# Slot stage: the normalisation ahead of attention, layers and gate moves from ScalarE (with shifts from VectorE) to GpSimd

## The reference

```python
slots = q_mu + jnp.exp(q_logsig) * noise          # noise = layernorm(x)
for _ in range(3):
    prev = slots
    q = _ln(slots, lnq_g, lnq_b) @ wq + bq         # norm "q"
    logits = jnp.einsum('bnd,bkd->bnk', k, q) / scale
    attn = jax.nn.softmax(logits, axis=-1) + 1e-8
    attn = attn / jnp.sum(attn, axis=1, keepdims=True)
    upd = jnp.einsum('bnk,bnd->bkd', attn, v)
    slots = upd @ wu + bu + prev
    h = _ln(slots, lnm_g, lnm_b) @ w1 + b1         # norm "m"
    slots = jax.nn.gelu(h) @ w2 + b2 + slots
    slots = _ln(slots + x_cls[:, None, :], lnp_g, lnp_b)   # norm "o"
...
x = x + slots
x = x + experts_b(_layernorm(x, axis=-1))          # norm "q" of a fourth round
```

## Time and profile before

| | |
|---|---|
| time, median of 3 runs | 892.08 us (891.86 to 893.96) |
| the profiled execution | 893.99 us, span of its instructions 892.1 us |
| busy in the span | PE 766.4 us, DVE 568.9, ACT 529.1, POOL 364.6 |
| busy, 700.8 to 743.5 us | PE 33.88, DVE 35.90, ACT 38.19, POOL 12.13 |
| mean granted TensorE clock | 0.918 of full speed |

### The profile page before, as it was taken

The page is one execution under the profiler, slowest core; times in us unless marked ns, Lnnn a source line. Parts: engine busy times, 40 slices in busy tenths (PEclk is TensorE's granted clock), DMA queues, the critical chain, the costliest instruction groups (busy, mean ns, idle before and its releaser), DMA issues.

```text
span 892.1 us, 17850 instructions
## 1 busy us (share of the span) xinstructions
PE 766.4 (86%) x5685; PEld 640.3 (72%) x5685; DVE 568.9 (64%) x1970; ACT 529.1 (59%) x1144; POOL 364.6 (41%) x571
## 2 busy tenths in 40 slices
PE   5989799999999999999988978999948787862793
PEld 4766687788887888777767656999836565752793
DVE  1657877788686667777765663343499888885012
ACT  3654567676666766666665542333549888851472
POOL 1323544343342334233336653565542232327362
PEclk9999999999999999999998979999957979785797
DMA  9424404360710520120232024888520000001674
GB/s 249 125 76 132 165 1 148 97 224 1 240 59 24 164 82 1 53 53 7 71 134 63 28 79 145 243 253 247 166 80 1 1 1 0 1 1 49 165 208 131
DMA packets 82054, 88.52 MB, mean 99 GB/s; under 512 B 6155, under 2 KB 69851, under 8 KB 81323
## 3 DMA queue, kind: packets, MB, share of 16 engines
q1 hardware_dynamic: 78475, 80.19, 30.3%
q0 software_dynamic: 3488, 7.20, 2.2%
HBM read 69.03 MB, written 35.17 MB: 117 GB/s over the span
## 4 chain that ended last, share of the span: by engine, by line
PE 58%; DVE 20%; ACT 9%; issue 5%; POOL 4%; DMA 3%; SPq 1%; DVEq 0%; POOLq 0%; ACTq 0%
PE bank L713 6%; PE bank L1036 6%; PE bank L707 5%; PE bank L740 4%; DVE sb_smax L1542 4%; PE bank L780 3%; DVE sb_row_sum L1551 3%; PE bank L1044 3%; PE bank L845 3%; PE bank L749 2%; PE bank L1145 2%; PE bank L765 2%; PE bank L1153 2%; POOL sb_expd L2066 2%; PE bank L722 2%
## 5 line engine op out<-in xcount | busy, mean ns | idle before, releaser
L2066 POOL TENSOR_TENSOR sb_expd<-sb_expd,sb_rden 128x512 f32<-128x512 f32 (+1 forms) x128 | 111.3, 870 | 248.4 <-DVE sb_rden L1555 248.3
L1542 DVE TENSOR_REDUCE sb_smax<-bank 128x4 f32<-128x512 f32 (+1 forms) x128 | 74.2, 580 | 75.9 <-PE bank L740 40.4
L1273 ACT ACTIVATE sb_expd<-sb_shifted 128x512 f32<-128x512 f32 (+1 forms) x128 | 69.7, 545 | 42.6 <-DVE sb_shifted L1545 41.6
L2158 POOL TENSOR_TENSOR sb_rstd_all<-sb_rsq_all,sb_halves 128x4 f32<-128x4 f32 x44 | 45.0, 1023 | 108.8 <-DVE sb_rsq_all L1893 108.6
L1551 DVE TENSOR_REDUCE sb_row_sum<-sb_expd 128x4 f32<-128x512 f32 (+1 forms) x128 | 73.0, 570 | 7.7 <-ACT sb_expd L1273 7.6
L1545 DVE TENSOR_TENSOR sb_shifted<-bank,sb_smax 128x512 f32<-128x512 f32 (+1 forms) x128 | 75.0, 586 | 4.4
L707 PE MATMUL bank<-sb_h1T,sb_watt 128*128 128x128 f32 x512 | 70.5, 289 | 4.6 <-DMA sb_watt<-att_w 2.9
L707 PEld LDWEIGHTS bank<-sb_h1T,sb_watt 128*128 128x128 f32 x512 | 64.6, 202 | 7.3 <-DMA sb_watt<-att_w 3.3
L1036 PE MATMUL bank<-sb_blk_xT,sb_up_w 128*128 128x128 f32 x456 | 57.1, 275 | 0.0
L1036 PEld LDWEIGHTS bank<-sb_blk_xT,sb_up_w 128*128 128x128 f32 x456 | 54.0, 192 | 0.0
L1855 DVE TENSOR_TENSOR sb_hid<-bank,sb_hid 128x384 f32<-128x384 f32 x38 | 21.2, 558 | 51.1 <-ACT sb_hid L1321 51.1
(11 more groups left out here) (285 smaller groups left out, 1997.9 us busy)
## 6 DMA issues: line engine op xcount, KB each, us to landing
sb_up_w<-gate_up SPq DMA_DIRECT2D x38, 384.0 KB, 4.3
sb_v<-v_all SPq DMA_DIRECT2D x16, 576.0 KB, 6.6
rows_b<-pad_b SPq DMA_DIRECT2D x7, 1105.0 KB, 10.1
rows_a<-pad_a SPq DMA_DIRECT2D x7, 975.0 KB, 8.3
sb_up_w<-w1b SPq DMA_DIRECT2D x23, 256.0 KB, 3.7
v_all<-sb_moe_w SPq DMA_DIRECT2D x14, 308.0 KB
sb_blk_x<-rows_a SPq DMA_DIRECT2D x38, 65.0 KB, 3.2
sb_picked<-back_a SPq DMA_DIRECT2D x4, 512.0 KB, 5.5
```

The costliest lines, as they stand in the source:

```text
L1273: act.activation(exp_of(i, s, j), shifted[:, u % 2, :, 0:n], ACT.Exp, scale=DH ** -0.5).then_inc(exp_done, 1)
L1542: dve.tensor_reduce(smax[:, u % 2, :], s_in, X, ALU.max).then_inc(max_done, 1)
L2066: pool.tensor_tensor(e, e, rden[:, u % 2, :].unsqueeze(2).broadcast_to([P, QH, n]), ALU.mult).then_inc(norm_done, 1)
```

## The change

The steps `norm_q` and `norm_m` leave ScalarE's queue for GpSimd's, and the steps `shift_q` and `shift_m` leave VectorE's altogether, with their semaphore. GpSimd waits for its own root and then runs one instruction a tile, (x - mean) * rstd, reading `mv_all` and `rstd_all` as per-partition scalars. TensorE waits for the same semaphore as before, now raised by GpSimd. The phases of `norm_q` and `norm_m` become those of their roots plus 0.0005, so each stands right behind its root in GpSimd's queue. No other phase changes. (Line numbers of the new kernel are its own: the root is L2137 there, the normalisation L2142, scaling L1354, exponentials L1365, shares L1371, Gelu L1377, bias L2150, scatter L2014.)

```diff
@@ SLOT_STEPS
-        "norm_q": (0.5900, 0.3921, 0.5369, 0.4138),
+        "norm_q": (-14.4877, -14.6377, -14.8345, -13.9260),
-        "norm_m": (2.9165, 2.4781, 2.0449, 2.1655),
+        "norm_m": (-12.5585, -11.6081, -12.5116, -12.9450),
@@ ScalarE
-            def normed(it, g, k, src, dst):
-                act.wait_ge(shift_ready[k], nth("shift_" + k, it, g))
-                for b in tiles(g):
-                    ins = act.activation(dst[:, b, 0:D], src[:, b, :], ACT.Identity, scale=rstd_all[:, b:b + 1],
-                                         bias=nbias[:, b:b + 1])
-                ins.then_inc(z_normed[k], 1)
@@ VectorE
-            def shifted_by(it, g, k):
-                c = slice(4 * g, 4 * g + 4)
-                dve.wait_ge(root_ready[k], nth("root_" + k, it, g))
-                dve.scalar_tensor_tensor(nbias[:, c], mv_all[:, c, 0], -1.0, rstd_all[:, c], ALU.mult, ALU.mult).then_inc(
-                    shift_ready[k], 1)
@@ GpSimd
-            for step, it, g in slot_steps("bias_u", "root_q", "root_m", "root_o", "send"):
+            def normed(it, g, k, src, dst):
+                pool.wait_ge(root_ready[k], nth("root_" + k, it, g))
+                for b in tiles(g):
+                    ins = pool.tensor_scalar(dst[:, b, 0:D], src[:, b, :], mv_all[:, b, 0:1], rstd_all[:, b:b + 1],
+                                             ALU.subtract, ALU.mult)
+                ins.then_inc(z_normed[k], 1)
+
+            for step, it, g in slot_steps("bias_u", "root_q", "root_m", "root_o", "send", "norm_q", "norm_m"):
...
+                if step == "norm_q":
+                    normed(it, g, "q", *((S, zs) if it < SLOT_ITERS else (x_sb, sent[0])))
+                if step == "norm_m":
+                    normed(it, g, "m", S, zs)
```

More of the change, by code:

```diff
@@ L492, in program @@
         var_ready, root_ready = ({k: sem(f"sl_{n}_{k}") for k in "qmo"} for n in ("var_ready", "root_ready"))
-        shift_ready, z_normed = ({k: sem(f"sl_{n}_{k}") for k in "qm"} for n in ("shift_ready", "z_normed"))
+        z_normed = {k: sem("sl_z_normed_" + k) for k in "qm"}
         zT_done, zT_ready = ({k: sem(f"sl_{n}_{k}") for k in "qm"} for n in ("zT_done", "zT_ready"))
@@ L1361, in scaled @@
                 act.activation(group_of(zsT, g), bank[2 * g][:, :], ACT.Identity, scale=scale, bias=bias).then_inc(zT_ready[k], 1)
-            for step, it, g in slot_steps("norm_q", "scale_q", "exp", "shares", "norm_m", "scale_m", "gelu", "choice_exp"):
-                if step == "norm_q":
-                    normed(it, g, "q", *((S, zs) if it < SLOT_ITERS else (x_sb, sent[0])))
+            for step, it, g in slot_steps("scale_q", "exp", "shares", "scale_m", "gelu", "choice_exp"):
                 if step == "scale_q" and it < SLOT_ITERS:
@@ L1381, in _ @@
                     ins.then_inc(att_ready, 1)
-                if step == "norm_m":
-                    normed(it, g, "m", S, zs)
                 if step == "scale_m":
@@ L1893, in measured @@
                 dve.scalar_tensor_tensor(rsq_all[:, 0, c], mv_all[:, c, 1], 1.0, eps[:, c], ALU.mult, ALU.add).then_inc(var_ready[k], 1)
-            def shifted_by(it, g, k):
-                c = slice(4 * g, 4 * g + 4)
-                dve.wait_ge(root_ready[k], nth("root_" + k, it, g))
-                dve.scalar_tensor_tensor(nbias[:, c], mv_all[:, c, 0], -1.0, rstd_all[:, c], ALU.mult, ALU.mult).then_inc(
-                    shift_ready[k], 1)
             of_b = [routing("b", part) for part in range(len(PARTS["b"]))]
             dve.wait_ge(exp_out["a"], len(PARTS["a"]) + 1)
-            for step, it, g in slot_steps("add", "measure_q", "shift_q", "max", "share_sum", "updated", "measure_m", "shift_m",
+            for step, it, g in slot_steps("add", "measure_q", "max", "share_sum", "updated", "measure_m",
                                           "measure_o", "centre", "slots", "gated", "choose", "place"):
@@ L1916, in _ @@
                     measured(g, x_sb, "q")
-                if step == "shift_q":
-                    shifted_by(it, g, "q")
                 if step == "max":
@@ L1938, in _ @@
                     measured(g, S, "m")
-                if step == "shift_m":
-                    shifted_by(it, g, "m")
                 if step == "measure_o":
```

## The result

The changed kernel takes 923.42 us (median of 4 runs, 917.5 to 925.31), against 892.08 before: a ratio of 1.0343 [1.03, 1.0386] with its 95% interval, 31 us slower and far outside the forecast range of 884.5 to 897.5. One further execution of the kernel before took 1126.62 us, far above all others, and is not counted. The changed kernel's profiled execution took 923.88 us with a span of 922.1.

What follows compares the result with a forecast made beforehand. No single engine was taken as full: four groups chase each other through four in-order queues. Laps -2.7, first delay +1.1 and tail +0.4 sum to -1.2 us, from 892.08 to 890.9 us; range 884.5 to 897.5.

Steps and rivals of the forecast that it cites:

- I take 0.40, nearer the upper row: Price of GpSimd's new instruction: 0.40 us a tile, chosen between a copy's 0.29 and a two-tensor addition's 0.45.
- I add nothing there: In a lap, a root delayed behind a normalisation on GpSimd costs nothing, since its slots run only at 740.35.
- likeliest case: Whole kernel: VectorE takes over what ScalarE lets go, change under 0.3%, 889.4 to 893 us; chance 0.40.
- first delay: Stage start: the first normalisation holds up the next group's output root on GpSimd, so VectorE's slots start later: +1.1 us.
- tail: Stage end: the last normalisation stands ahead of GpSimd's twelve scatters, so loads of scattered rows start later: +0.4 us.
- the laps' -2.7: Slot-loop laps: Gelu on ScalarE no longer waits behind the normalisation, 0.9 us gained at each of three lap ends.
- faster rival: Whole kernel: a tile costs 0.30 us and more of ScalarE's relief arrives, -5 us, 887; chance 0.33.
- dear instruction: GpSimd: at 0.90 us a tile a group takes 3.6 us and GpSimd becomes the bound: +7 us, 899; chance 0.15.
- Seven paths 1 us longer: Slow case at 0.90 us a tile: seven normalisation paths each lengthen by 1 us.
- It decides from about 0.65 a tile: GpSimd price from which the slow case holds: a path is as long as the mean now and roots queue.
- instructions that fall under a normalisation: VectorE: some 6 small instructions a lap wait a mean of 0.2 us for GpSimd, 1.2 us, even with removed shifts.
- a rival of its own: VectorE's slots also alternate with GpSimd's tiles, 11 hits of up to 0.4 us a lap: +4.5 us, 895; chance 0.12.

Runs made afterwards that it cites:

- run 4: Not a name in the kept text: "median of 4 runs" only counts the timed runs of the changed kernel, 923.42 us.
- second experiment: Kernel before, normalisations still on ScalarE, with GpSimd also running four tiles of the new instruction on unread data behind each such root: 920.78 us, 1.0348.
- subtraction kernel: Changed kernel with one subtraction of two 128x128 tensors a tile on GpSimd, the multiplication left out: 893.97 us, 1.001.
- Two tiles: Kernel before with two tiles of each normalisation on GpSimd by the change's instruction, two left on ScalarE: 891.78 us, 1.0004.
- copy kernel: Changed kernel with a plain copy of each tile on GpSimd in place of the normalisation: 886.29 us, 0.9941.
- three-tile one: Kernel before with three tiles of each normalisation on GpSimd by the change's instruction, one left on ScalarE: 903.58 us, 1.014.
- wide products: Changed kernel with two broadcast two-tensor instructions on 512 elements a group in place of four tile instructions on GpSimd: 902.77 us, 1.0119.
- one tile: Kernel before with only the last tile of each normalisation on GpSimd, three left on ScalarE: 890.18 us, 0.998.
- the shifts alone: Kernel before with only the shifts moved from VectorE to GpSimd, as two 128x4 products: 890.3 us, 0.9987.

## Why the prediction was wrong

**The first failed step is the price**: "I take 0.40, nearer the upper row" and "a group of four costs 1.6 us". It is 0.80 and 3.13 (813 ns mean in the changed kernel, 792 alone). The nearest rows were other kinds: the one reads a tensor and computes nothing, the other computes on two tensors, and both lie below what GpSimd needs for a tensor and a scalar, even a constant (565). The bound of 0.90 "by its kind" held it; the choice between the ends, by how much an instruction reads, did not. But the price is not the whole error: at 0.90 a tile the prediction's own working gave +7 us, and the change costs 31.

**The second is the queue**: of the roots that stand behind a normalisation in a lap it said "I add nothing there". At 3.13 us a group, GpSimd's tiles and roots have 52% of the chain of the stage, and filling the queue alone, with no path changed, costs 31 us (second experiment).

**With that price the total came near, its terms less so.** The forecast of -1.2 us was for a group of 1.6; the subtraction kernel, at 1.5, gave +0.9 [-1.1, +2.8]. That is inside the forecast's range for its likeliest case, with -1.2 itself just outside the interval. (Two tiles, at 1.6, gave +0.4, but leave half of the work on ScalarE.) By the subtraction kernel's trace the first delay was right: its second root starts 2.63 us after the first (653.91 and 651.28), 2.69 by the forecast, 1.39 before. The tail was too small: +2.05 us for +0.4. It took the last scatter to land at 824.9, 1.4 us ahead of the loads; but from the start of the last scatter to the loads it is 3.7 us before, and 4.1 to 4.2 in the subtraction and the changed kernel, so the slack there was about half a microsecond. And the laps' -2.7 is not to be seen: to the last root the stage is 164.7 us long, against 163.9 and 165.5 before, where -2.7 and +1.1 would make it 1.6 shorter. That too small a cost and too large a gain still ended near the sum is partly luck. The faster rival asked for 0.30 a tile and said -5; the copy kernel has 0.30 and -5.3, of which 2.0 to 3.6 lie in the stage. The bounding, "four groups chase each other through four in-order queues", was right as well: the copy kernel took 10.5 us of the steady stretch off ScalarE (27.67 for 38.19) and gained 0.6%.

**Where "dear instruction" was right and too small.** Its price was close (0.90 against 0.80), its place too, and its +7 was too small by more than a factor of four. The three parts that it names add up to 12.5; the 5.5 taken off as "a little relief" have no row. By its parts:
- "Seven paths 1 us longer". The chain from 650 to 812 us has 18 normalisations and 27 roots. The count was taken from the chain of before, in which a normalisation rarely comes; but a chain is that of one schedule, and a queue that fills becomes the chain.
- The roots behind the tiles. "I add nothing there", it said of the root at 736.18, on the ground that its slots run 4 us later. That slack was for one normalisation of 1.6 us ahead. At 3.13, and with three groups in a row, the root that starts at 748.31 lies behind 12.7 us of solid work. The idle tiles show that such waiting behind tiles is enough for the whole 31 us.
- "The first delay 3.1, the tail 2.4". The first output root now starts 656.00, was 653.35; the slots 657.14, were 654.58: 2.6 later, 2.9 from the stage's first root. The tail, from the last root to the loads, is 3.9 longer. These two, 6.8 us, were close to size; the 25 us between them were missed.
- "It decides from about 0.65 a tile", 2.6 us a group. In the medians the loss begins between 1.6 and 2.4 us, 0.4 to 0.6 a tile; by the stage's own length it may have begun at 1.6. And "41 us of work in a lap of 42.7" looked for a bound at full load; GpSimd is at 74% in the changed kernel, 69% in the three-tile one, which already loses 12 us. At 60% (two tiles) the median loses nothing.

**Exclusion.** The forecast had VectorE lose as much to "instructions that fall under a normalisation" as it saves on shifts, and a rival of its own for it. The variance's mean is 165 ns in the changed kernel, where the earlier trace rows had its like at 0.16: next to nothing is lost to tiles with two scalars. The rule of the Trainium skill ("SBUF — State Buffer", "Who interferes with whom"), that a VectorE instruction with two SBUF inputs and any GpSimd one that reads SBUF shut each other out, shows here only for GpSimd's products of two tensors: 447 ns under the wide ones, in line with the 1.02 us of the earlier trace rows. By the trace it is narrower than it is written. How much of the wide products' 10.6 us comes from it was not separated: a straight line between the points without it, at 1.6 and 2.4 us a group, gives 8 us of queueing at 2.1, and less if the curve bends upward there as it does further on. The variance took 19.7 us in all there against 7.1, so up to 12.6 us of VectorE's queue.

**What would have shown it.** Of the marks named, ScalarE's fall to about 25 us came (22.61), the output root after the first normalisation came at 656.00 for 654.6, the mean above 0.65 failed the sum, and "GpSimd's roots queueing" stands among those of a wrong forecast. The loads of the scattered rows do wait for the last scatter now (2.5 us). Two marks failed: VectorE's idle time before the measurement of a lap's sums is still there (6.1 us in all for 5.2), and no maximum of the small instructions came near 0.5 us (0.21 for the variance, 0.37 behind the maximum).

**No version beats the kernel before.** The nearest are one tile or the shifts alone, 0.998 and 0.9987, both with intervals that take in no change or touch it. The copy kernel, which leaves the arithmetic out, gains 0.6% (0.3 to 0.9); no instruction measured here does the work at a lower price, so in this order of steps that is the most that such a move of all four tiles can be expected to give. Whether other phases would make room for it was not tried.

## What to carry to other kernels

An instruction of a kind that an engine never runs in the trace has no near row: subtraction and multiplication with two scalars on GpSimd cost 0.80 us, where the rows taken for nearest had 0.29 and 0.45. Measure it in a tail of the kernel before building a sum on it. When work goes to an idle engine whose queue also holds tiny instructions that others wait for (here one root of 1.02 us for each measurement), price the queue, not the path: what counts is how long one visitor holds it up against the slack of what stands behind, and how many come in a row. Here the cost could be told from somewhere between 60 and 69% load. A copy of the work on data that nobody reads, as in the second experiment, prices the queue alone.

## What the runs showed of the hardware

On GpSimd, a 128x128 float tile costs 291 ns to copy, 396 to combine with another tensor or a broadcast column, 565 with one constant and 792 with two per-partition scalars. At 512 elements a partition they are 613, 1038, 1487 and 2072. By the difference of the two sizes, each further element costs 0.84, 1.67, 2.40 and 3.33 ns. So one operation with a per-partition scalar is dearer than the same kind with that scalar as a broadcast tensor (602 for 396): two such products (two times 396) come to the price of the one fused instruction, 792.

GpSimd's wide operations on two tensors held up a small VectorE instruction with two SBUF inputs (447 ns in the mean for one of 0.16 us, up to 0.90); GpSimd's operation of a tensor with two scalars, and its copy, hardly did (165 and 172 in the mean).
